# Feature turns, token mixtures and the first products of the scan stage: a rounding split over two engines, four-deep rings, an early W_in

## The reference, cut to what matters

```python
# block one, per batch of 1024 tokens, 16 heads of 16 channels
p  = einsum('blhd,dm->blhm', q or k, proj_mat) / 4          # 128 projections per head
qp, kp = concat([cos(p), sin(p)]) / sqrt(128)               # the features
kv = einsum('blhm,blhd->bhmd', kp, v)
attn = einsum('blhm,bhmd->blhd', qp, kv)
xr = mu_r * x + (1.0 - mu_r) * x_prev                       # the two mixtures
xk = mu_k * x + (1.0 - mu_k) * x_prev
r = sigmoid(xr @ W_r.T); k_act = square(relu(xk @ W_k.T)); g = r * (k_act @ W_v.T)
# block two, first half: the scan, per batch, 512 channels, 16 states
xi, z = split(x @ W_in.T); u = silu(conv4(xi) + conv_b)
dt = softplus(...);  h = h * exp(dt * A) + (dt * u) * B_t;  y = sum_s(h * C_t)
```

## Time and profile before

| | us |
|---|---|
| median of 3 runs | 2482.49 (2481.26 to 2482.85) |
| the profiled execution | 2483.26 |
| its span, first to last instruction | 2481.1 |
| mean granted TensorE clock | 0.938 of full speed |

### The profile page before, as it was taken

How to read it: one execution, slowest core, us unless ns; L and a number is a source line. 1 busy time by engine, 2 the same in 40 slices (tenths; PEclk the granted TensorE clock), 3 DMA queues, 4 the chain that set the end, 5 groups by cost and what they waited for, 6 DMA issues and landing times. The chain is left out here.

```text
span 2481.1 us, 24432 instructions
## 1 busy us (share of the span) xinstructions
PE 1995.6 (80%) x7355; PEld 1006.8 (41%) x7371; DVE 1646.6 (66%) x2303; ACT 1264.7 (51%) x1703; POOL 1082.0 (44%) x605
## 2 busy tenths in 40 slices
PE   4789778967886796879978988998776669989883
PEld 3326433633463253323324332433232236655552
DVE  4754576366726533379989998999899962225663
ACT  3962586268527731466654665466544424434441
POOL 3001201020111010178888898989877751213553
PEclk9899899989999998989998998999999999999996
DMA  7410730073016202488888888988889972223444
GB/s 173 108 34 0 184 72 18 13 189 70 0 38 164 53 34 62 7 286 287 291 288 284 300 275 279 298 289 276 273 274 345 328 255 79 90 89 90 122 122 131
DMA packets 183457, 407.69 MB, mean 164 GB/s; under 512 B 49937, under 2 KB 78865, under 8 KB 182114
## 3 DMA queue, kind: packets, MB, share of 16 engines
q1 hardware_dynamic: 171298, 375.31, 50.3%
q0 software_dynamic: 12032, 30.82, 4.3%
HBM read 360.50 MB, written 49.70 MB: 165 GB/s over the span
## 5 line engine op out<-in xcount | busy, mean ns | idle before, releaser
L1150 POOL TENSOR_TENSOR late<-late,rows 128x1024 f32<-128x1024 f32 x256 | 603.2, 2361 | 153.6 <-DVE late L1623 148.4
L1760 PE MATMUL m_Q<-late,ident_m 128*128 128x512 f32 x1024 | 527.7, 646 | 170.7 <-POOL late L1150 118.2
L1623 DVE TENSOR_TENSOR_SCAN late<-m_Q,late 128x1024 f32<-128x1024 f32 x256 | 586.3, 2290 | 47.5 <-ACT m_Q L1324 19.5
L1324 ACT ACTIVATE m_Q<-late,acol 128x1024 f32<-128x1024 f32 x256 | 286.0, 1117 | 373.9 <-DVE late L1623 373.7
L1760 PEld LDWEIGHTS m_Q<-late,ident_m 128*128 128x128 f32 x1024 | 193.1, 201 | 478.2 <-POOL late L1150 281.7
L1616 DVE TENSOR_TENSOR late<-m_Q,rows 128x1024 f32<-128x1024 f32 x256 | 307.3, 1200 | 40.5 <-ACT m_Q L1330 34.5
L424 DVE SCALAR_TENSOR_TENSOR early<-early,work 128x1024 f32<-128x1024 f32 x128 | 156.0, 1219 | 123.1 <-ACT early L570 122.3
L1507 ACT ACTIVATE late<-m_Q,e_b1c 128x128 f32<-128x128 f32 x312 | 89.2, 369 | 202.4 <-PE m_Q L1825 173.2
L302 POOL TENSOR_TENSOR xk<-kr 128x1024 f32<-128x1024 f32 x8 | 15.0, 1894 | 397.3 <-DVE kr L438 397.3
L570 ACT ACTIVATE early<-work,rnd 128x1024 f32<-128x1024 f32 x128 | 141.7, 1110 | 63.2 <-PE work L722 60.0
L1837 PE MATMUL m_Q<-rows,late 128*128 x624 | 155.8, 393 | 21.3 <-ACT late L1507 12.5
(11 more groups left out here) (226 smaller groups left out, 3086.5 us busy)
## 6 DMA issues: line engine op xcount, KB each, us to landing
rows<-bc_s SPq DMA_DIRECT2D x512, 512.0 KB, 5.5
stack<-st_s SPq DMA_DIRECT2D x64, 384.0 KB, 5.8
st_s<-qkh SPq DMA_DIRECT2D x128, 96.0 KB, 2.4
r_s<-late SPq DMA_DIRECT2D x39, 256.0 KB
stack<-st_s SPq DMA_DIRECT2D x32, 256.0 KB, 6.7
xin<-in_x SPq DMA_DIRECT2D x4, 1024.0 KB, 9.9
xres<-in_x SPq DMA_DIRECT2D x4, 1024.0 KB, 7.5
mx_s<-s SPq DMA_DIRECT2D x4, 1024.0 KB, 4.5
```

Source lines behind the costliest of these rows:

```text
L1150: nc.gpsimd.tensor_tensor(pr[:, n % NH, :], h[:, n % NH, :], cb[:, n % NCB, :], ALU.mult).then_inc(pr_ok, 1)
L1324: A(dA[:, :], dt[:, (b * KI + m) % 2, :], ACT.Exp, scale=acol[:, m, i % NS:i % NS + 1]).then_inc(dA_ok, 1)
L1623: v_.tensor_tensor_scan(h[:, n % NH, :], dA[:, :], dB[:, n % 2, :], 0.0, ALU.mult, ALU.add).then_inc(h_ok, 1)
L1760: ins = mm(half(Y, c), ident[:, :], half(pr[:, n % NH, :], c), start=False, stop=(n % NS == NS - 1), skip_group_check=True)
```

## The change

- `phase_a`: `fs` and `fc` become rings of four turns, with `key_sums` and `attend` three turns behind the projection (`KLAG`). In 13 of the 32 turns (3, 5, 8, 10, 12, 14, 17, 20, 22, 25, 27, 29, 31) VectorE does the rounding, from PSUM with a tensor_scalar, and ScalarE does it in the other 19.
- The mixtures go to GpSimd, as four tensor_scalar and two tensor_tensor of 128x1024 for each of the two, ahead of the bias on `xn_a`.
- VectorE takes `r` and `kk` out of PSUM ahead of its part of turns 15, 19, 22 and 28 and not behind it; the transposes of the key sums come later, and `sums` are used in the other order by `attend`.
- Last batch: the four `x` products of the scan's first batch run in `phase_a` behind the feed-forward (`mx`), into a buffer `xi4`; `FIRST` then begins with the convolutions. `count(0)` follows `conv 1`. `bc` is accumulated tile by tile as the `u` tiles come (`first_rows`).
- The first tile's dt*u is made by VectorE behind `route`, in two operations, straight into `du`.
- `DRIVE` becomes steps 8, 10, 12, 12; softplus and `rate` of each batch's fourth tile move one step earlier.
- `stack`, `aT`, `xk` and `xi4` share one SBUF region with the scan stage's rows.

```diff
+NF_ = 4
+TURNED = (9, 13, 17, 20)
+AHEAD = 1
+KLAG = 3
+ACT_ROUNDS = tuple(s for s in range(32) if s not in (3, 5, 8, 10, 12, 14, 17, 20, 22, 25, 27, 29, 31))
...
+                def mixture(b, i):
+                    dst = (xr, xk)[i]
+                    for k in range(KD):
+                        nc.gpsimd.tensor_scalar(dst[:, k, :], xnT[:, k, 0:L], omu[:, i, k:k + 1], None, ALU.mult).then_inc(part_ok, 1)
+                        nc.gpsimd.tensor_scalar(aT[:, k, :], xnT[:, k, 1:L + 1], cols[:, 6 + i, k:k + 1], None, ALU.mult).then_inc(part_ok, 1)
+                    for k in range(KD):
+                        pool.wait_ge(part_ok, (b * 2 + i) * 2 * KD + 2 * k + 2)
+                        nc.gpsimd.tensor_tensor(dst[:, k, :], dst[:, k, :], aT[:, k, :], ALU.add).then_inc(mix_ok, 1)
...
                 for b in range(B):
                     pool.wait_ge(tr_ok, b * 6 + 4)
+                    if b:
+                        pool.wait_ge(lg_ok, b)
...
+                    mixture(b, 0)
+                    mixture(b, 1)
                     pool.wait_ge(x2_ok, b * TB + TB)
                     add_bias(xn[:, :, :], 1, TB, xb_ok)
...
+                    def whole_turns(s):
+                        job = ("kf", s) if s < 16 else ("qf", s - 16)
+                        wait_full(dv, b, *job)
+                        if s >= NF_:
+                            dv.wait_ge(feat_used, b * 32 + s - NF_ + 1)
+                        v_.tensor_scalar(fs[:, s % NF_, :], slot(b, *job)[:, :], ROUND, None, ALU.add).then_inc(turns_v, 1)
...
-                        if 4 <= s < 4 + 4 * KD:
-                            mix(b, link, s - 4)
...
+                        if s not in ACT_ROUNDS:
+                            whole_turns(s)
...
+                    for s in range(AHEAD):
+                        whole_turns(s)
                     for s in range(32):
-                        if s < 31:
-                            whole_turns(s + 1)
+                        if s + AHEAD in ACT_ROUNDS:
+                            whole_turns(s + AHEAD)
...
-                        u = s - 2
+                        u = s - KLAG
...
                     if last:
+                        pe.wait_ge(g["m_in_ok"], 16)
+                        pe.wait_ge(g["m_x_in"], 16)
+                        for m in range(2 * KD):
+                            by_channel(b, ("mx", m), w_in, xT)
                         normed(b)
...
-DRIVE = (10, 13, 13, 14)
+DRIVE = (8, 10, 12, 12)
...
                 route()
+                dv.wait_ge(soft_ok, 2)
+                v_.tensor_tensor(dt[:, 0, :], dt[:, 0, :], soft[:, :], ALU.add).then_inc(dt_ok, 1)
+                dv.wait_ge(dt_ok, 1)
+                dv.wait_ge(silu_ok, tile_at(0, "conv", 0) + 1)
+                v_.tensor_tensor(du[:, :], dt[:, 0, :], u[:, 0, :], ALU.mult).then_inc(du_ok, 1)
                 times_b(0)
...
+                def first_rows():
+                    for k in range(KI):
+                        pe.wait_ge(silu_ok, tile_at(0, "conv", k) + 1)
+                        for c in range(NC_):
+                            at = AT[0, "bc", 0, c]
+                            if k == 0:
+                                pe.wait_ge(x_read, at - 1)
+                            ins = mm(X[at % 2][0:2 * NS + DR, :], w_bc[:, k, :], half(u[:, k, :], c),
+                                     start=(k == 0), stop=(k == KI - 1), skip_group_check=True)
```

More of the change, by code:

```diff
@@ L35 @@
 TAKEN = {15: ("r", 0), 19: ("r", 1), 22: ("kk", 0), 28: ("kk", 1)}
+NF_ = 4
[3 more added lines that the diff above has]
+ACT_ROUNDS = tuple(s for s in range(32) if s not in (3, 5, 8, 10, 12, 14, 17, 20, 22, 25, 27, 29, 31))
+BY_ACT = [sum(s in ACT_ROUNDS for s in range(n)) for n in range(33)]
+BY_DVE = [n - BY_ACT[n] for n in range(33)]
 PRE = [("t", i) for i in range(4)] + [("k", 0), ("k", 1), ("v", 0), ("q", 0), ("q", 1), ("v", 1)]
@@ L55, in sequence @@
         n = [(b + 1, j) for j in PRE] if b + 1 < B else []
+        if not n:
+            seq += [(b, ("mx", m)) for m in range(2 * KD)]
         seq += n[0:8] + [(b, ("xn", 0)), (b, ("xn", 1))] + n[8:9] + [(b, ("gl",))] + n[9:] + [(b, ("gate",))]
@@ L601, in batch @@
                     if last:
+                        for m in range(2 * KD):
+                            wait_full(ac, b, "mx", m)
+                            A(xi4[:, m, 3:3 + L], slot(b, "mx", m)[:, :], ACT.Identity).then_inc(mx_ok, 1)
                         normed(b)
@@ L776, in besides @@
                             by_channel(b, ("kk", i), wkk, xk, pieces=(int(second),))
-                    for s in range(32 + 2):
+                    for s in range(32 + KLAG):
                         if s < 32:
@@ L915, in phase_me @@
         early = g["early"]
-        rows = sb("rows", [P, 4 * 2 * L])
+        rows = g["rows"]
+        xi4 = rows[:, 0:KI * (DC - 1 + L)].rearrange("p (m t) -> p m t", m=KI)
         late = sb("late", [P, 10 * L])
@@ L1189, in _ @@
                     silu(0, "conv", m)
-                rate(0)
-                drive(0)
                 pool.wait_ge(rt_ok, 1)
@@ L1462, in _ @@
                     softplus(0, link)
-                drive_out(0)
                 for b in range(B):
@@ L1771, in _ @@
                 for kind, m, c in FIRST:
-                    for piece in range(PIECES[kind]):
-                        half_job(0, kind, m, c, piece)
-                    if (kind, m, c) == ("x", 3, 1):
+                    if (kind, c) == ("bc", 0):
+                        first_rows()
+                    elif kind != "bc":
+                        for piece in range(PIECES[kind]):
+                            half_job(0, kind, m, c, piece)
+                    if (kind, m, c) == ("conv", 1, 1):
                         count(0)
@@ L1881, in blocks @@
     with ExitStack() as ctx:
-        for name, shape in (("early", [P, 8 * L]), ("lg", [P, NT, E]), ("w_bc", [P, KI, 2 * NS + DR]), ("w_dt", [DR + 1, DI]), ("acol", [P, KI, NS]),
+        for name, shape in (("early", [P, 8 * L]), ("rows", [P, 8 * L]), ("lg", [P, NT, E]), ("w_bc", [P, KI, 2 * NS + DR]), ("w_dt", [DR + 1, DI]), ("acol", [P, KI, NS]),
                             ("taps", [P, KI, DC]), ("vecs", [P, 2, KI]), ("one", [P, 1]), ("ident_m", [P, P])):
```

145 lines of the change are left out of this document (78 added, 67 removed), and 2 rows, old and new, of the table FILL.

## The result

| | before | after |
|---|---|---|
| median, us | 2482.67 (4 runs, 2481.26 to 2493.47) | 2377.86 (4 runs, 2370.31 to 2380.76) |
| ratio, 95% interval | | 0.9564 [0.9529, 0.9599] |
| the profiled execution, its span | 2483.26, 2481.1 | 2378.56, 2376.7 |

The medians alone give 0.9578; the table's ratio is that of the means, in which the run of 2493.47 counts.

What follows compares the result with a forecast made beforehand. ScalarE was taken to bound block one's serial loops (at least 96 of 118.3 us). Loops 62, end of block one 2.4, scan start 26 and tile changes 21 make 111 off 2483.3: 2372 us, range 2342 to 2415.

Steps and rivals of the forecast that it cites:

- ScalarE loses 13 roundings: 96 - 13 = 83 us.: Block one's loop: 32 turns need at least 96 us on ScalarE; giving 13 roundings to VectorE leaves 83.
- The layout by hand: Batch 1's loop, turns laid out instruction by instruction: last sine ends at 101.8 us against 118.2, gain 16.4 a batch.
- The lock: Loop: VectorE's absolute values wait for GpSimd's instructions; gain 16.4 us a batch, near 25 without any loss by it.
- wide-lock rival: Loop: one-input mixtures cost 2.35 us or misses queue for two turns; loops gain 24, total 2410; chance 20%.
- In the key half the lock eats all of the gain of about 10 us: Loop up to turn 12: its sines start at 44.1 us after the first rounding, 44.0 before.
- the slow path of the last rival: Loop: GpSimd's one-input column product is slow, duration p; equals old loop plus other gains from p = 8.3; 4%.
- `stack` hidden: Loop: DMAs into `stack` land some 6 us after issue and are needed over 10 us later, so cost nothing.
- The start of the scan: From the barrier to the first scan: 78.6 us becomes 52; 26 gained, bounds 18 and 29.
- The changes of tile: Scan: all seven waits for `drive_out` and the echoes behind them go, less a remainder; 21 us gained, bounds 12 and 25.
- their echoes on the decay behind them, 7.8: Scan, changes of tile: waits for decays behind the `drive_out` waits would also go, 7.8 us.
- late-drive rival: Scan: the early drive moves GpSimd's lateness to the products with C; the 21 us are lost, total 2393; 8%.
- End of block one: Behind the last loop: the `mx` products fill TensorE's wait for the norm; 2.4 us gained, bounds 0 to 4.

Runs made afterwards that it cites:

- experiment 1: Changed kernel with other GpSimd mixtures: batch 1 multiplies by a constant, batch 2 works on 8 columns only, batch 3 copies; 2367.95 us in one run.
- experiments 1 and 2: Experiment 1, and from the second the changed kernel with all 32 roundings on ScalarE again: 2380.46 us, ratio 0.9573, loop 102.5.
- experiment 6: Changed kernel with `r` copied at turn 14, 1 MB loads behind `stack` units, bias rows behind first rows of B and C: 2364.71 us, ratio 0.9541.
- experiment 5: Changed kernel with the steps of the scan's drive as before, loops and start as changed: 2389.87 us, ratio 0.9613.
- the last one: Changed kernel with three moves, VectorE rounding 6 turns, not 13, and a difference shared by both GpSimd mixtures: 2347.84 us, ratio 0.9540.

## Why the prediction was right, and where it was not

The time and the loops' 58 us were right. The reason that I gave for the loops was not, and that the number came so near is in part luck.

**"ScalarE loses 13 roundings: 96 - 13 = 83 us."** This is the step that failed. I read ScalarE's 97.5 busy us of 118.3 as what bounds the loop, so the split was to free it. With all roundings back on ScalarE the loop takes 102.5. A share of 82% isn't a bound: 21 us were idle, and the question was who ended them. With the copies ahead and nothing else, ScalarE is as busy as before and the loop takes 109.0. I had the row: 60 us of ScalarE's idle time ended with a projection of TensorE. I did not ask what TensorE waited for. It waited for PSUM tiles that VectorE had still to copy out, 11.3 us in batch 1. The layout by hand gave 101.8 all the same; I take it that this is because it followed the new lists, with the copies where they now stand, which no run can show. So the sum was right for an edit that the sum doesn't name.

**The lock.** The price of a mixture multiplication is 2.84, not 1.1, and lies beyond the upper end that I kept. By the wide-lock rival that should have cost 38 us. It didn't, because the price of being held is the remainder of one instruction, and most absolute values came near an end. Batch 1's first 14 absolute values, 13 of them under the mixtures and the bias, take 16.0 where 14 x 0.69 is 9.7 (the expectation of experiment 1 has 8.6), so they are held for 6.3, against a price of 4.4 to 6.0 in the period. Being stretched ended not at turn 8 but at turn 12 (2.53). "In the key half the lock eats all of the gain of about 10 us" gave the right start of turn 12 for the wrong reason. Without the lock the key half gains 5, not 10, and with the lock but all roundings on ScalarE it gains 3.3 (experiments 1 and 2). The layout also had the sines of turn 6 at 25.3, and they started at 21.0. From there to turn 12 the trace has 6.5 us for `stack` that the layout left out, though with 1.4 of them left turn 12 starts at 43.0 as well (experiment 6). An instruction priced too low, hits priced too high and a wait that was missing came out even: that is the luck. In kind the slow path of the last rival came true, with a p of 2.84, too short to cover the loop.

The Trainium skill's "GPSIMD Engine Reference", section "Elementwise — side-by-side cycle accounting", has 1.03 cycles per element for a light one-input body, which the prediction turned into an estimate of 0.88 us plus dispatch. The copy agrees with that (1.04), the multiplication doesn't (2.84), and the measurement decides.

**`stack` hidden.** Wrong: 6.5 us of TensorE at turn 8. I took 6 us from issue to landing, and left out that the two loads ahead of it in the same queue move 2 MB; the last of the unit's three DMAs took 11.6 to land (12.3 in batch 2), and 6.3 with the loads behind it (experiment 6). In the loop it cost little: with it and a copy's wait nearly gone the loop gained 1.2.

**The start of the scan.** 24.0 for 26. `route` ended 45.4 behind the barrier, and the forecast had 43 to 47: right. Softplus ended 49.1 behind the barrier, at the late end of 46.4 to 49. But I gave `route` only VectorE's queue to stand in. SyncE's queue holds the bias rows until `route` ends, and behind them the store of B and C: the rows of B came 1.7 late. Moving them gave 1.6.

**The changes of tile.** 15.1 for 21. All waits for `drive_out` went, as worked out, and all of it by these steps (experiment 5). The term that was too large is "their echoes on the decay behind them, 7.8". Waits for decays didn't fall, they went from 19.5 to 21.7, such as 0.83 and 2.33 at the change at 1328, and those for the rows of B rose by 1.1: 17.9 - 2.2 - 1.1 = 14.6 of the 15.1. In the trace GpSimd is behind with its products at that change, TensorE's `add_state` waits for them, and the next filler product and ScalarE's evacuation of it come late. That is the late-drive rival at under a third of its price; the chain is read off the trace, not tested.

**End of block one**: 3.3 for 2.4, within its bounds. The 4.1 in the expert stage I can't explain, and they may be nothing but spread: the stretch behind the sixteenth gate takes 453.8 before and 449.6 after, and 446.3 to 454.1 in the other traces but the last one's, which is from a faster chip; its work is the same in all. The granted clock was 0.93 after and 0.94 before, which speaks the other way.

## What to carry to other kernels

A busy share says who could be the bound; the idle rows of the busiest engine say who is. Follow them one engine further before pricing an edit: here ScalarE waited for TensorE, and TensorE for a PSUM tile that VectorE read 2 us later than it could have. Where a ring of three PSUM tiles is shared by a long chain and a side job, take the side job's tile out first in the turn: here that alone, with no instruction added or removed, took 33 us off the old kernel. And when an expected number comes true, undo the edit that is said to have made it.

## What the runs showed of the hardware

- GpSimd on 128x1024 float32: copy 1.04 us, 1.50 when it reads from the second column on; multiplication by a constant 2.77, by a column 2.84; addition of two tensors 2.56 in the mixtures and 2.35 for the bias of `v`; a difference of two slices of one tensor 2.1.
- GpSimd and a VectorE absolute value (SBUF to SBUF) hold each other back: 2.84 becomes 3.31 where one ran between, and VectorE's 0.69 became 2.53 at worst in the changed loop of batch 1 (4.97 in batch 3, under the bias of 128x2048). VectorE's rounding and subtraction, which read PSUM, show 1.20 to 1.23 in all 180 instances, under GpSimd's instructions too.
- DMAs into `stack`: a median of 5.8 us to landing for the four of 384 KB issued between 284 and 305. The one of 256 KB behind them took 11.6 (12.3 in batch 2) when 2 MB of loads had been issued just ahead in the same queue, and 5.9 for the next unit.
